# PSUM as two first-in-first-out rings, and where the small products stand in a two-layer transformer kernel

## What is computed

```python
x = x + attn0(layernorm(x))   # 16 heads of 8 channels; softmax(q @ k.T * scale) @ v, then a projection
x = x + ffn0(layernorm(x))    # (silu(x @ w_gate.T) * (x @ w_up.T)) @ w_down.T, 384 hidden channels
x = x + attn1(layernorm(x))   # the same attention, with an RMS norm over each head of q and of k
x = x + ffn1(layernorm(x))    # x @ base.T + b + 2 * sum_e gating[e] * (x @ A) @ B[e], gating = softmax(x @ router.T)
```

## Time and profile before

| | |
|---|---|
| median of 3 runs | 2136.7 us (2132.09 to 2147.0) |
| the profiled execution, its time and its span | 2135.92 us, 2134.1 us |
| slots of the loop, X of sequence 3 to Y of sequence 13, 11 passes | 405.4 to 1776.0 us of the span |
| PE, DVE, ACT, POOL busy, share of the span | 86%, 75%, 67%, 20% |
| granted TensorE clock, mean | 0.934 of 2.4 GHz |

### The profile page before, as it was taken

How to read it: one execution, slowest core, us unless ns; L and a number is a source line. 1 busy time by engine, 2 the same in 40 slices (tenths; PEclk the granted TensorE clock), 3 DMA queues, 4 the chain that set the end, 5 groups by cost and what they waited for, 6 DMA issues and landing times.

```text
span 2134.1 us, 38850 instructions
## 1 busy us (share of the span) xinstructions
PE 1831.3 (86%) x10958; PEld 688.9 (32%) x10958; DVE 1598.7 (75%) x3593; ACT 1432.2 (67%) x2921; POOL 432.8 (20%) x570
## 2 busy tenths in 40 slices
PE   4858989888988988888898888989898998998775
PEld 1232323333332333333333333323333332333322
DVE  4538888887878778778787878777787878888471
ACT  2716686776767677677766767676776768776543
POOL 2112131221212122121212212120121213121200
PEclk9957999999999999999999999999999999999867
DMA  5203223050413205041320504123050413212020
GB/s 109 71 11 101 47 67 96 18 140 17 118 34 96 65 17 140 17 115 37 81 81 17 140 17 115 36 71 91 17 140 17 115 37 79 79 35 59 29 53 16
DMA packets 162647, 140.87 MB, mean 66 GB/s; under 512 B 38761, under 2 KB 144050, under 8 KB 162482
## 3 DMA queue, kind: packets, MB, share of 16 engines
q1 hardware_dynamic: 162482, 139.29, 24.7%
HBM read 77.38 MB, written 55.57 MB: 62 GB/s over the span
## 4 chain that ended last, share of the span: by engine, by line
PE 37%; issue 24%; DMA 11%; ACT 9%; POOL 8%; DVE 8%; SPq 3%; ACTq 0%; POOLq 0%; DVEq 0%
PE ps L1127 11%; PE ps L1112 7%; PE ps L1148 5%; ACT probs L647 5%; DVE neg_max L853 4%; PE ps L1102 4%; DMA k_stack<-k_rows 4%; DMA rden_all<-rden_rows 3%; PE ps L1078 3%; PE ps L1153 2%; PE ps L1191 2%; DMA k_rows<-kp 2%; PE ps L1141 2%; POOL o_raw L551 2%; POOL qk L561 2%
## 5 line engine op out<-in xcount | busy, mean ns | idle before, releaser
L853 DVE TENSOR_REDUCE neg_max<-ps 128x1 f32<-128x512 f32 x2048 | 1316.4, 680 | 196.8 <-PE ps L1102 167.7
L647 ACT ACTIVATE probs<-ps 128x512 f32<-128x512 f32 x2048 | 1093.4, 599 | 324.5 <-PE ps L1112 309.0
L1102 PE MATMUL ps<-k_stack,q_stack 48*128 48x512 bf16 x2048 | 702.5, 402 | 86.6 <-DVE neg_max L853 46.4
L1112 PE MATMUL ps<-q_stack,k_stack 50*128 50x512 bf16 x2048 | 655.1, 391 | 79.8 <-ACT probs L647 75.7
L1127 PE MATMUL ps<-probs,v_aug 128*32 128x512 f32 x4096 | 568.1, 628 | 1.0
L1112 PEld LDWEIGHTS ps<-q_stack,k_stack 50*128 50x128 bf16 x2048 | 150.8, 95 | 525.1 <-ACT probs L647 342.4
L1102 PEld LDWEIGHTS ps<-k_stack,q_stack 48*128 48x128 bf16 x2048 | 159.3, 94 | 280.3 <-DVE neg_max L853 239.4
L551 POOL TENSOR_TENSOR o_raw<-o_raw,rden_all 128x512 f32<-128x512 f32 x64 | 81.3, 1270 | 569.6 <-DMA rden_all<-rden_rows 569.6
L1127 PEld LDWEIGHTS ps<-probs,v_aug 128*32 128x32 f32 x4096 | 81.7, 109 | 136.3 <-issue 81.5
L1153 PE MATMUL ps<-wo,o_raw 128*128 128x128 f32 x512 | 81.8, 326 | 43.2 <-POOL o_raw L551 43.1
L653 ACT ACTIVATE xn<-x,shift,rstd 128x128 f32<-128x128 f32 x192 | 80.5, 484 | 52.4 <-POOL shift L534 52.4
(11 more groups left out here) (103 smaller groups left out, 1499.4 us busy)
## 6 DMA issues: line engine op xcount, KB each, us to landing
q_stack<-q_rows SPq DMA_DIRECT2D x128, 192.0 KB, 3.7
k_stack<-k_rows SPq DMA_DIRECT2D x128, 192.0 KB, 4.6
rden_all<-rden_rows SPq DMA_DIRECT2D x64, 256.0 KB
q_rows<-qp SPq DMA_DIRECT2D x32, 384.0 KB, 2.6
k_rows<-kp SPq DMA_DIRECT2D x32, 384.0 KB, 2.9
q_rows<-qp SPq DMA_DIRECT2D x32, 256.0 KB, 3.0
k_rows<-kp SPq DMA_DIRECT2D x32, 256.0 KB, 3.0
x_in<-in_L_attn_x SPq DMA_DIRECT2D x16, 256.0 KB, 2.8
```

The lines of the kernel that those rows point to most:

```text
L647: act.activation(probs[:, u % RING, :], ps[:, bank_of(l, u), :], ACT.Exp).then_inc(exps, 1)
L853: dve.tensor_reduce(neg_max[l][:, pair // 2, col:col + 1], ps[:, BANKS + bank_of(l, n), :], AX.X, ALU.max, negate=True).then_inc(max_taken, 1)
L1102: pe.matmul(ps[:, BANKS + bank_of(l, m), :], q_stack[l][row:row + KROWS, pair, tok:tok + 128], k_stack[l][row:row + KROWS, pair, :], start ...
L1112: pe.matmul(ps[:, bank_of(l, u), :], k_stack[l][row:row + AROWS, pair, tok:tok + 128], q_stack[l][row:row + AROWS, pair, :], start=True, s ...
```

## The change

PSUM is dealt out as two rings in order of use. Four banks (0, 1, 2, 6) are the ring of all that ACT reads: attention units and the pieces `xt*`, `q0`, `k0`, `qt`, `kt`, `m*`, `g*`, `ct`. Three banks (3, 4, 5) are the ring of all that DVE reads: maxima units and the pieces in `TO_VECTOR`. Bank 7 is the accumulator; `gen` is gone. Two pairs of semaphores (`a_full`, `a_free`, `v_full`, `v_free`) count every use, and a table worked out ahead gives each item its bank, the count that frees it, and its own count. Pieces are placed by half-step, and `pr0`, `pr1`, `dn` and `out` are issued in two parts in neighbouring half-steps. `q0`, `k0` and each `g` and `u` are one product of 512 columns in place of two of 256. In the gate stage ACT reads `g` twice (tanh and a copy), DVE makes `(th + 1) * u` from the bank of `u`, and POOL multiplies with the copy of `g`. Several ACT, DVE and POOL items move by one or more half-steps, and sequence 2 is now unrolled (`LOOP_FROM` 3).

```diff
-BANKS = 3
-X_PE = ((1, "xt0"), (3, "q0"), (4, "m01"), (5, "k0"), (7, "qt"), (8, "kt"), (11, "pr1"), (12, "m02"), (14, "v1"),
-        (19, "xt3"), (20, "m03"), (21, "rt"), (27, "ct"), (28, "m10"), (29, "out"))
-Y_PE = ((4, "m11"), (7, "v0"), (9, "pr0"), (12, "m12"), (13, "xt1"), (14, "g0"), (15, "u0"), (16, "g1"),
-        (17, "u1"), (18, "g2"), (19, "u2"), (20, "m13"), (21, "dn"), (25, "xt2"), (26, "qka"), (27, "qkb"),
-        (28, "m00"))
+A_BANKS, V_BANKS = (0, 1, 2, 6), (3, 4, 5)
+ACC_BANK = 7
+X_PE = ((1, "xt0"), (5, "q0"), (7, "k0"), (10, "m01"), (11, "qt"), (14, "kt"), (17, "v1"), (22, "pr1"), (26, "m02"),
+        (40, "xt3"), (42, "m03"), (44, "rt"), (55, "ct"), (58, "m10"), (60, "out"))
+Y_PE = ((10, "m11"), (13, "v0"), (19, "pr0"), (26, "m12"), (28, "xt1"), (30, "g0"), (31, "u0"), (32, "g1"),
+        (34, "u1"), (35, "g2"), (36, "u2"), (41, "dn"), (43, "m13"), (50, "xt2"), (53, "qka"), (55, "qkb"),
+        (58, "m00"))
+HALVES = {"pr0": 2, "pr1": 2, "dn": 2, "out": 2}
+TO_VECTOR = ("v0", "v1", "pr0", "pr1", "u0", "u1", "u2", "dn", "qka", "qkb", "rt", "out")
...
-LOOP_FROM, LOOP_TO = 2, BATCH - 2
+LOOP_FROM, LOOP_TO = 3, BATCH - 2
...
+        for ring, key, _, _, _ in items:
+            banks = A_BANKS if ring == "A" else V_BANKS
+            bank[key] = banks[place[ring] % len(banks)]
+            place[ring] += 1
+            freed[key] = held[bank[key]] if bank[key] in held else 0
+            held[bank[key]] = done[key]
...
-            def gate_tanh(c, b):
-                act.wait_ge(written[f"g{c}"], b + 1)
-                act.activation(th[:, :], gen, ACT.Tanh, scale=0.5).then_inc(tanh_done, 1)
-
-            def take_up(c, b):
-
-                act.wait_ge(written[f"u{c}"], b + 1)
-                copy(up[:, :], gen).then_inc(read[f"u{c}"], 1)
+            def take_gate(c, b):
+                act.wait_ge(a_full, done_at(f"g{c}", b))
+                need(act, ht_done, NH * b - NH + c + 1)
+                act.activation(th[:, c, :], ps[:, bank_at(f"g{c}", b), :], ACT.Tanh, scale=0.5)
+                copy(gate[:, c, :], ps[:, bank_at(f"g{c}", b), :]).then_inc(a_free, 1)
...
                         if "M2" in have:
-                            if s == 7:
-                                take_qk(1, 0, i - 1)
-                                take_part0(1, 0, i - 1)
-                            if s == 8:
-                                take_qk(1, 1, i - 1)
-                            if s == 9:
-                                take_part0(1, 1, i - 1)
-                            if s in (10, 11):
-                                take_part1(1, s - 10, i - 1)
+                            if h in (11, 14):
+                                take_qk(1, (h - 11) // 3, i - 1)
+                            if h in (12, 15):
+                                take_part0(1, (h - 12) // 3, i - 1)
+                            if h in (16, 19):
+                                take_part1(1, (h - 16) // 3, i - 1)
...
-                            if h < 11:
-                                inverse_rms(3 + h, 1, i - 1)
-                            if h in (29, 30):
-                                take_v(1, h - 29, i - 1)
+                            if h < 7:
+                                inverse_rms(7 + h, 1, i - 1)
+                            if h == 17:
+                                take_v(1, 0, i - 1)
+                                take_v(1, 1, i - 1)
...
-                            if h == 11:
+                            if h == 10:
                                 invert_den(1, 1, i - 2)
...
-                need(pe, max_taken, free_at(l, m, b, base))
+                need(pe, v_free, freed_before("max", l, m, b))
...
-                need(pe, exps, free_at(l, u, b, UNITS * attends_before(l, b)))
+                need(pe, a_free, freed_before("exp", l, u, b))
...
-            def piece(name, k, i, at, kind, b):
-                before = piece_before(kind, at, name)
-                if k == 0 and before is not None:
-                    pe.wait_ge(read[sem_name(before[0])], count(before[0], i + before[1]))
+            def piece(name, k, b):
+
+                bank = bank_at(name, b)
+                free, full = (v_free, v_full) if name in TO_VECTOR else (a_free, a_full)
+                if k == 0:
+                    need(pe, free, freed_before(name, b))
+                tiles = range(TT) if span(name) == 1 else (2 * k, 2 * k + 1)
...
-                    for q, name, k, last in plan:
-                        if q == h:
-                            op = piece(name, k, i, at, kind, i + PIECE[name][0])
-                            if last:
-                                op.then_inc(written[sem_name(name)], 1)
+                    for at_half, name in pieces:
+                        if 0 <= h - at_half < span(name):
+                            piece(name, h - at_half, i + PIECE[name][0])
```

495 lines of the change are left out of this document (254 added, 241 removed).

## The result

The changed kernel is slower: 2275.1 us, median of 4 runs (2269.1 to 2277.4), against 2134.4 (2127.5 to 2147.0) of the kernel before on the same chip, a ratio of 1.065 [1.059, 1.070]. The forecast was 2040, range 1975 to 2112, and slower by more than 1% had a chance of 0.08. The profiled execution took 2277.4 us; its span is 2275.6.

A forecast was written before the change was run, and what follows sets the result against it. It took DVE as the bound, idle 25.4 us of each 124.6 us pass. Terms of -6.2 us a pass over 14 passes (-87), with savings outside them, made -96 us, for 2040 us, range 1975 to 2112.

The forecast's parts named there:

- ACT's block: Slot X: ACT's earlier cast waits for POOL's residual, new DVE idle time of +2.2 us a pass, bounds 0 and +4.
- the forecast's -6.2 us a pass: Sum of the terms over a whole loop pass, counted for 14 passes as -87 us.
- One loop branch fewer is -2: Loop branch: one turn fewer saves 2 us in the whole run.
- rival 2: Slot X: ACT's wait for the residual outlasts both rings' store, all engines stand; 2164 us, chance 0.05.
- `pr0`: Slot Y: pr0 hangs on a chain that grows as m11 moves later; +0.4 us a pass after its two parts.
- Bursts, -5.4: DVE's waits ahead of maxima: fewer pieces start behind a value product, -5.4 us a pass, bounds 0 and -10.8.
- rival 1: Idle time only moves: DVE's smaller ring store and fixed chains eat the bursts' gain; 2103 us, chance 0.20.
- Two parts, -2.4: Splitting dn, out and pr1 shortens DVE's waits for them: -2.4 us a pass, bounds -1.2 and -5.0.
- Gate stage: DVE's wait for the tanh shrinks, -1.0 us a pass; sequence 0's stage falls from 20.2 to 14.4 us, -6.
- DVE's own instructions are the same: DVE in the loop: same instructions in number and kind, so a pass can't fall below 99.2 us.
- my mark of 0.93: Granted clock in the loop, counted as unchanged from 0.96; below 0.93 the forecast would be wrong.
- Rival 3: PE's clock: more small gaps bring more stretches at 1.2 GHz and eat the gain; 2136 us, chance 0.05.

The follow-up runs named there:

- e1_pad: The changed kernel with extra satisfied PE waits ahead of the loop, so only where the loop's body begins differs: 2242.4 us.
- e6_pool: e2_unroll with both first residuals of layer 1's q and k ahead of the normalisation in POOL's slot X queue: 2100.9 us, 0.988 of the kernel before.
- e7_m8: e6_pool with the small pieces m01 and m11 at half-step 8 in place of 10: 2074.6 us, 0.975 of the kernel before.
- e2_unroll: The changed kernel written out without a loop: 2173.7 us, 1.018 of the kernel before.
- e5_bunroll: The kernel before written out without a loop: 2076.8 us, 0.976 of the kernel before.
- e14_loop: The changed kernel, loop kept, with e1_pad's waits, e6_pool's POOL order and m01, m11 at half-step 8: 2110.9 us, 0.991 of the kernel before.
- e15_long: The kernel before with satisfied PE waits added, giving the changed kernel's loop body length (1677 instructions) and place: 2264.6 us, 1.057 of the kernel before.
- e16_long2: The kernel before with e15_long's body of 1677 PE instructions, moved to e1_pad's place: 2241.9 us, 1.047 of the kernel before.
- e9_whole: e7_m8 with pr0, pr1, dn and out whole, not in halves, and DVE's four additions one half-step earlier: 2063.9 us, 0.968 of the kernel before.
- e8_ring: e7_m8 with the fourth bank given to DVE's ring, leaving ACT three: 2077.5 us, 0.974 of the kernel before.
- e13_both: e7_m8 with m13 earlier, xt2, qka, qkb and their readers later, plus e9_whole's edit: 2045.3 us, 0.958 of the kernel before.

## Why the prediction was wrong

**The account.** The changed kernel lost 141 us: 33 to the fetches (e1_pad), 73 to ACT's block (e6_pool), 26 to SP's queue (e7_m8). The loop's other cost is 11 us higher (e1_pad to e2_unroll 69, kernel before to e5_bunroll 58, or 53 with the kernel before on e5_bunroll's own chip), though it has one pass fewer; the longer register arithmetic may be in that, which no run tests. What is left of the change itself, e7_m8 against e5_bunroll, is -2: +17 in the passes and about -20 outside. So with all three causes gone the forecast's -6.2 us a pass is +1.5, and +0.2 with whole pieces. The terms add up by way of the unrolled kernels; in the loop, e14_loop gives a larger sum for the two queues.

**"One loop branch fewer is -2", and no word on the turn.** I took the turn as it was and looked only at what the engines do in it. The change made PE's body 104 instructions longer (141 more of register arithmetic), and that, with where the body begins, brought a stall of 3.3 us at each turn. The 1.2 GHz behind the turn was there before. No term and no rival had it, though the trace of before showed queue q8 with 28 packets, all outside the passes, and the two programs' loops could be counted. Shown by e1_pad, e15_long and e16_long2.

**ACT's block: right mechanism, wrong price and wrong part of the chain.** I put +2.2 us a pass, bounds 0 to +4; it cost 5.3 (e6_pool). ACT's wait was as foretold (4.4, "3 to 5"), DVE's idle time at h = 20 was 4.0 in the changed kernel ("about 2"). Two things failed. The sentence of rival 2 that "the chain's parts are POOL operations and two DMAs whose times the change does not touch": the chain also goes through SP's queue, where `m01` had come to stand between the reciprocal and its line, so it took 10.6 us in place of 8.1 (means 10.6 and 8.3). I had written just that for `pr0` and not asked it in slot X. And I counted a stall at its own length: all engines stood, the clock fell to 1.2 GHz, and the PE rows behind it took up to twice their time (mean clock of the eight half-steps 0.78, and 1.00 in e6_pool). The rival gave "+8.4 a pass" as the point from which it decides; alone it did not reach that.

**`pr0`: right mechanism, mis-sized.** The term was +0.4. Y 16-23 grew by 2.1 us, with a wait of 2.36 and both halves at 1.2 GHz, and "PE waiting 2 us or more" came true. The 0.6 us of `m11` wasn't the size: with `m11` at 8 the same stretch is 1.9 us shorter.

**Bursts, -5.4: didn't come.** With the other causes gone DVE waits 155.5 / 11 = 14.1 us a pass ahead of maxima, against 8.3 in the kernel before without its loop: +5.8. In e9_whole it is 106.8 / 11 = 9.7, so 4.4 of the 5.8 come with the halves and their later additions; what remains is +1.4 in place of -5.4. That is rival 1's outcome, idle time that only moves. Its mechanism, the smaller store of DVE's ring, isn't borne out: with a fourth bank (e8_ring) the wait for maxima stayed at 155.7 us. Which part of the new placing takes back the gain stays open. `k_stack` was no longer waited for, as foretold.

**Two parts, -2.4: the rows came true, the gain did not.** Waits of `dn` fell from 2.7 to 0.8 us a pass ("under 2"), those of the projections from 5.3 to 3.7. The profile showed each wait that I had named getting shorter, and e9_whole, which takes back the halves and the additions' places together, shows that this was worth less than nothing: what the additions no longer wait, the maxima wait, and more.

**Gate stage.** In the passes DVE's wait was 15.3 us for the tanh and is 16.0 for the `u` product: 0, not -1.0. In sequence 0 the forecast was 14.4 us and it took 10.8, from the first of these rows to the second:

```profile
125.32 2.05 PE L1232 MATMUL ps<-xnt,w_gate 128*128 128x512 f32 x2 [0.78 <-ACT xnt L684]
...
136.14 1.58 PE L1238 MATMUL ps<-w_down,ht 128*128 128x128 f32 x12 [0.44 <-POOL ht L624]
```

The prediction took each of the six products at 2.07 us, which is their time at 1.2 GHz. The whole stage ran at that clock before (0.50); now it does so only up to 131 us, and the last `u` takes 1.02 us. The stage gave 9.4 us in place of 6, and that it gave more is luck: the clock's rise was in no term.

**"DVE's own instructions are the same."** In number and kind, yes. But the cast behind each 16th maximum went from 175 to 311 ns in the mean, 12 us in 11 passes. Its median is 175 ns in both kernels. In 33 of the 88 cases a POOL operation is running when the cast starts, and then the cast ends 28 to 34 ns behind it, as in these rows; in the kernel before none of the 88 meets one.

```profile
1346.63 1.27 POOL L608 TENSOR_TENSOR o_raw<-o_raw,rden_all 128x512 f32<-128x512 f32 x1 [6.43 <-DMA rden_all<-rden_rows]
...
1347.60 0.34 DVE L907 CAST neg_high<-neg_max 128x16 bf16<-128x16 f32 x1
```

So the new places of POOL's work cost DVE 1.1 us a pass, which the floor of 99.2 us left out.

**The clock.** 0.91 was below my mark of 0.93. Rival 3 took the rings' small gaps as the cause. In the Trainium skill, in the section that the prediction names beside this rival (TensorE: Matmul & The Clock Gate, "A second HAM failure mode: psum-queue depth-cycling"), such gaps let the clock go back and forth. Here they aren't what lowered it: with the same rings e7_m8 has 0.97 and e13_both 0.98. The clock is low behind the long common stalls, in slot X at h = 20, at `pr0` and behind the turn, and it recovers in X 16-23 when that stall goes (0.77 in e2_unroll, 1.00 in e6_pool).

## What to carry to other kernels

Before the places of a loop's work are changed, look at how long the loop's body is on each engine and at the instruction fetches in the trace, and look again after: a body that just fitted can stop fitting through a hundred register instructions, or through what stands ahead of the loop. When a consumer is moved earlier, follow what it waits for through every queue, and ask of each operation ahead of it in the queue whether it has to be there. A stall of all engines can cost more than its length (3.6 us at h = 20 cost 5.3), but need not: the 3.3 us at the turn cost 3.3 (e1_pad), and the 9.0 us a pass of e16_long2's added waits cost 8.4. And a single wait that gets shorter is no gain until the idle time of the bounding engine, over the whole pass, has fallen.
